# A two-layer graph kernel: every block transposed on VectorE, 2 MB loads in 1,024-byte runs, interleaved row sets

## The reference, cut to what matters

```python
def L0(x, evals, evecs, t):                    # evecs is adj, 4096 x 4096
    x_spec = einsum('nk,nc->kc', evecs, x)     # adj^T x
    coefs = exp(-evals * clip(t[0], 1e-8))[:, None]
    return einsum('nk,kc->nc', evecs, coefs * x_spec)   # adj (coefs * adj^T x)
def L1(inputs, adj, W, b):
    adj_hat = adj + eye(N)
    return tanh((adj_hat / adj_hat.sum(1)) @ (inputs @ W) + b)
x = layernorm(x + L0(x, evals, adj, t))        # x: 4096 x 128, float32
x = layernorm(x + L1(x, adj, W, b))
```

## Time and profile before

| | |
|---|---|
| median of 3 runs | 701.69 us (701.64 to 701.8) |
| the profiled execution, its own time | 704.87 us |
| its span | 703.1 us |
| busy: PE, DVE, ACT, POOL | 636.9, 516.4, 407.2, 341.6 us |
| DMA, whole span | 176.82 MB, 251 GB/s |

### The profile page before, as it was taken

The page is one execution under the profiler, slowest core; times in us unless marked ns, Lnnn a source line. Parts: engine busy times, 40 slices in busy tenths (PEclk is TensorE's granted clock), DMA queues, the critical chain, the costliest instruction groups (busy, mean ns, idle before and its releaser), DMA issues.

```text
span 703.1 us, 9318 instructions
## 1 busy us (share of the span) xinstructions
PE 636.9 (91%) x3016; PEld 518.7 (74%) x3016; DVE 516.4 (73%) x648; ACT 407.2 (58%) x825; POOL 341.6 (49%) x167
## 2 busy tenths in 40 slices
PE   3899999999958779899998999999999799898983
PEld 3688888887747558677786888888888587777862
DVE  3699899998949787868774356465528589698975
ACT  4899999999944555535453435346325364554540
POOL 0000000002916677664929848767927738373751
PEclk9999999999988999999998999999999899999997
DMA  8999999999999999897969759788749789999900
GB/s 290 387 386 386 387 387 387 387 387 387 332 248 248 231 270 220 237 190 216 252 155 274 172 128 241 179 180 241 184 115 267 152 224 262 240 264 266 255 16 30
DMA packets 198582, 176.82 MB, mean 251 GB/s; under 512 B 6280, under 2 KB 147848, under 8 KB 198544
## 3 DMA queue, kind: packets, MB, share of 16 engines
q1 hardware_dynamic: 124080, 137.90, 65.3%
q10 hardware_dynamic: 74464, 38.43, 24.8%
HBM read 174.21 MB, written 2.10 MB: 251 GB/s over the span
## 4 chain that ended last, share of the span: by engine, by line
PE 49%; POOL 13%; DVE 12%; ACT 10%; issue 7%; DMA 4%; ACTq 4%; SPq 0%; POOLq 0%; DVEq 0%
POOL lo L320 11%; PE ps L659 10%; PE ps L661 10%; PE ps L660 10%; ACT hi L358 7%; PE ps L652 5%; DMA raw<-in_adj_dram 4%; PE ps L630 4%; PE ps L632 4%; PE ps L631 4%; DVE vt L474 3%; DVE lo L482 3%; ACTq L261 3%; ACT hi L373 2%; POOL rstd L315 1%
## 5 line engine op out<-in xcount | busy, mean ns | idle before, releaser
L320 POOL TENSOR_TENSOR lo<-vt,hi 128x1024 fp32r<-128x1024 f32 x119 | 296.8, 2524 | 166.9 <-ACT hi L373 166.9
L474 DVE STREAM_TRANSPOSE vt<-raw 128x1024 f32<-128x1024 f32 x138 | 167.8, 1229 | 58.8 <-PE ps L661 57.6
L373 ACT ACTIVATE hi<-vt 128x1024 fp32r<-128x1024 f32 x138 | 142.2, 1057 | 71.5 <-DVE vt L474 50.6
L455 DVE TENSOR_TENSOR lo<-raw,hi 128x1024 fp32r<-128x1024 f32 x120 | 154.4, 1287 | 21.6 <-ACT hi L358 19.1
L358 ACT ACTIVATE hi<-raw 128x512 fp32r<-128x512 f32 x256 | 158.5, 622 | 14.4 <-DMA raw<-in_adj_dram 8.7
L373 ACT ACTIVATE hi<-ps 128x1024 fp32r<-128x1024 f32 x62 | 63.4, 1028 | 116.1 <-PE ps L652 114.1
L659 PE MATMUL ps<-hi,s_hi 128*128 128x512 f32 x256 | 108.7, 425 | 8.2 <-POOL lo L320 7.9
L482 DVE TENSOR_TENSOR lo<-ps,hi 128x1024 fp32r<-128x1024 f32 x62 | 75.0, 1211 | 54.2 <-ACT hi L373 54.1
L630 PE MATMUL ps<-hi,xg_hi 128*128 128x512 f32 x256 | 102.8, 402 | 9.5 <-DVE lo L455 8.7
L659 PE MATMUL ps<-hi,p_hi 128*128 128x512 f32 x256 | 105.4, 412 | 4.2 <-POOL lo L320 3.1
L308 POOL TENSOR_TENSOR lo<-raw,hi 128x1024 fp32r<-128x1024 f32 x8 | 25.4, 3197 | 169.4 <-ACT hi L358 169.3
(11 more groups left out here) (60 smaller groups left out, 611.3 us busy)
## 6 DMA issues: line engine op xcount, KB each, us to landing
raw<-in_adj_dram SPq DMA_DIRECT2D x95, 1024.0 KB, 14.2
raw<-in_adj_dram SPq DMA_DIRECT2D x138, 256.0 KB, 5.6
raw<-in_adj_dram ACTq DMA_DIRECT2D x138, 256.0 KB, 6.4
out_dram<-o_g ACTq DMA_DIRECT2D x8, 256.0 KB, 3.7
x_sb<-in_x_dram SPq DMA_DIRECT2D x1, 1792.0 KB, 14.7
x_sb<-in_x_dram SPq DMA_DIRECT2D x1, 256.0 KB, 3.3
w_sb<-in_L_gnn_W_dram ACTq DMA_DIRECT2D x1, 64.0 KB, 6.1
b_bc<-in_L_gnn_b_dram ACTq DMA_DIRECT2D x1, 64.0 KB, 8.0
```

What stands on the lines that cost most here:

```text
L320: nc.gpsimd.tensor_tensor(lo[:, slot(p), :], vt[:, slot(p), :], hi[:, slot(p), :].bitcast(f32), ALU.subtract).then_inc(pool_lo_ready, 1)
L373: nc.scalar.activation(hi[:, slot(s), :], src, ACT.Copy).then_inc(hi_ready, 1)
L455: nc.vector.tensor_tensor(lo[:, q % RING1, :], raw[:, k, 2 * h:2 * h + 2, :].rearrange("p r n -> p (r n)"), hi[:, q % RING1, :].bitcast(f3 ...
L474: nc.vector.transpose(vt[:, slot(s), :].rearrange("p (m b i) -> p m b i", m=2, b=RB), raw[:, BLOCKS[n].buf].rearrange("p r w -> p (r w)") ...
```

## The change

Five things change together. (1) PE transposes no block of adj any more: DVE transposes all 200 steps, and lo of every step is made from `vt` in SBUF, by DVE for 55 steps and by POOL for 145. (2) Loads are of 2 MB: 512 rows by 1,024 columns, 52 of them for 100 blocks, in 3 buffers in place of 6 of 1 MB, in runs of 1,024 bytes. Where only one half of the columns is needed (rows of odd groups in stage 3, four times), the whole 2 MB are loaded. (3) A row group takes every other set of 32 rows of 1,024 rows, and a column unit every other set of 32 columns of 1,024, so `x`, `out` and the spectrum are laid out anew; x is loaded by 8 DMAs. (4) All loads of adj are issued by SP, four quarters in a row. (5) Stage 3 writes its results over `x_sb`, without the buffer `o_g` and its wait. Besides, in the last visit of stage 1 POOL makes lo of 4 of the 16 halves, not of 8, and the spectrum is transposed in pairs of chunks, the last pair behind the products of step 1. The row groups are taken from 0 up.

```diff
-    BY_TENSOR = (0, 1)
-    RAW_RING = 6
+    BUFS = 3
+    WQ = 2 * CW // QN
...
     def on_vector(s):
-        if block(s).by_tensor:
-            return True
-        n = V_STEPS.index(s)
-        return n % 4 == 3 if block(s).spectral and block(s).visit < 4 else n % 6 == 5 and not block(s).spectral
+        if STEP[s].spectral:
+            return s % 16 in (2, 5, 8, 11, 14) if STEP[s].group < 3 else s % 4 == 2
+        return s % 7 in (2, 5)
...
+    LATE_POOL = [q for q in range(PAIRS) if q % 4 == 1]
+    LATE_DVE = [q for q in range(PAIRS) if q % 4 != 1]
...
-    adj_q = adj.rearrange("(g b n) (k q w) -> g k q n b w", b=RB, n=QP, q=QN, w=P)
+    adj_q = adj.rearrange("(v a e n) (u q w) -> v e u q n a w", v=NU, e=2, n=QP, q=QN, w=WQ)
...
-            for n in range(NB):
+            for n in range(NL):
                 wait_buffer(sp, n)
-                if BLOCKS[n].by_tensor:
-                    sp.dma_start(raw[:, BLOCKS[n].buf], adj_v[group(BLOCKS[n].visit), BLOCKS[n].col])\
-                        .then_inc(raw_in[BLOCKS[n].buf], 16)
-                else:
-                    load_quarters(sp, n, (0, 1))
+                load_quarters(sp, n, range(QN))
...
             def hi_step(s):
-                wait_turned(act, s)
+                act.wait_ge(vturned, s + 1)
                 wait_slot(act, s)
-                src = turn_slot(s).rearrange("p a n -> p (a n)") if block(s).by_tensor else vt[:, slot(s), :]
-                nc.scalar.activation(hi[:, slot(s), :], src, ACT.Copy).then_inc(hi_ready, 1)
-                n = AFTER.get(s // 2)
-                if s % 2 == 1 and n is not None and not BLOCKS[n].by_tensor:
-                    load_quarters(act, n, (2, 3))
+                nc.scalar.activation(hi[:, slot(s), :], vt[:, slot(s), :], ACT.Copy).then_inc(hi_ready, 1)
...
-            for p in range(1, POSITIONS):
-                if p + AHEAD < STEPS and not block(p + AHEAD).by_tensor:
+            for p in range(AHEAD, POSITIONS):
+                if p + AHEAD < STEPS:
                     turn_step(p + AHEAD)
...
+            def spectrum(u):
+                pe.wait_ge(spec_out, 2 * u + 2)
+                for c in range(2 * JB):
+                    last = nc.tensor.transpose(ps[:, 2 * u + c // JB, c % JB * C:(c % JB + 1) * C],
+                                               spec[:, u % 2, c * P:(c + 1) * P], ident[:, :])
+                last.then_inc(sT_done, 1)
...
-            for p in range(2, POSITIONS):
-                if p < STEPS and block(p).by_tensor:
-                    turn_step(p)
+            for p in range(AHEAD, POSITIONS):
                 if 0 <= p - LAG < STEPS:
                     products(p - LAG)
+                if p - LAG == 1:
+                    spectrum(NU - 1)
```

More of the change, by code:

```diff
@@ L7 @@
 @dataclass(frozen=True)
-class Block:
-    visit: int
-    col: int
+class Load:
+    group: int
+    wide: int
     buf: int
-    by_tensor: bool
+@dataclass(frozen=True)
+class Step:
+    load: int
+    last_of_load: bool
+    group: int
+    unit: int
+    half: int
     spectral: bool
@@ L90, in spectral_then_graph_conv, with wides2 @@
[L90 to L100, removed]
+    def wides2(g):
+        newest = (g - 1) // 2 if g else NU - 1
+        known = [u for u in range(NU) if 2 * u + 1 < g and u != newest]
+        unknown = [u for u in range(NU) if 2 * u + 1 >= g and u != newest]
+        order = []
+        while known or unknown:
+            if unknown:
+                order.append(unknown.pop(0))
+            if known:
+                order.append(known.pop(0))
+        return order + [newest]
@@ L102, in on_vector @@
+    NL = len(LOADS)
+    STEP = [Step(n, w == WORK[n][-1] and half == 1, LOADS[n].group, w[0], half, w[1], w[2], w[3])
+            for n in range(NL) for w in WORK[n] for half in range(2)]
+    STEPS = len(STEP)
+    BEFORE = [next((m for m in range(n - 1, -1, -1) if LOADS[m].buf == LOADS[n].buf), None) for n in range(NL)]
+    LAST_STEP = [max(s for s in range(STEPS) if STEP[s].load == n) for n in range(NL)]
     def on_vector(s):
-        if block(s).by_tensor:
-            return True
-        n = V_STEPS.index(s)
@@ L114, in spectral_then_graph_conv @@
     LO_BY_POOL = {s: i + 1 for i, s in enumerate(POOL_LO)}
-    END2 = [max(s for s in range(STEPS) if block(s).spectral and block(s).visit == v) for v in range(NG)]
-    END3 = [max(s for s in range(STEPS) if block(s).row == r) for r in range(NG)]
+    LATE_POOL = [q for q in range(PAIRS) if q % 4 == 1]
+    LATE_DVE = [q for q in range(PAIRS) if q % 4 != 1]
+    END2 = [max(s for s in range(STEPS) if STEP[s].spectral and STEP[s].group == g) for g in range(NG)]
+    END3 = [max(s for s in range(STEPS) if STEP[s].row == r) for r in range(NG)]
@@ L570, in ending3 @@
                         dve.wait_ge(sumT_done, row - 1)
-                    nc.vector.tensor_tensor(stage[:, par, :], acc_row(row), save(v), ALU.add).then_inc(sum3, 1)
+                    nc.vector.tensor_tensor(stage[:, par, :], acc_row(row), save(g), ALU.add).then_inc(sum3, 1)
                 if since == 2:
@@ L663, in products @@
             def products(s):
-                bl = block(s)
-                v = bl.visit
-                first = FIRST[v, bl.row] == s
-                final = s == (END2[v] if bl.spectral else END3[bl.row])
+                st = STEP[s]
+                g = st.group
+                first = FIRST[g, st.row] == s
+                final = s == (END2[g] if st.spectral else END3[st.row])
                 wait_lo(pe, s)
-                if bl.spectral and v == 0:
-                    pe.wait_ge(s_ready, max(bl.col + 1, 5))
```

411 lines of the change are left out of this document (181 added, 230 removed).

## The result

The change makes the kernel slower: 853.74 us (median of four runs, 847.89 to 859.4) against 701.66 beside it, a ratio of 1.217 (95% interval 1.207 to 1.227). Forecast were 690 us, in a range of 674 to 718. The profiled execution took 849.83 us with a span of 848.0.

A forecast was written before the change was run, and what follows sets the result against it. PE was taken to bound late stage 2, POOL's stalls its earlier visits, PE and DVE stage 3. Handover -4, stage 2 -18 and stage 3 +10 gave -12: 704.9 becomes 693, the median 690 us, range 674 to 718.

The forecast's parts named there:

- Stage 1 ... is the same program over the same 2,048-byte runs, and I leave it at no change.: Stage 1 before 170 us, limited by its loads: same program and run length, so no change in time.
- A packet of 1,024 bytes then costs 44 to 75 ns, a load 5.6 to 9.6 us; I take 7.5.: Loads in stage 3: 7.5 us each against 4 steps of 2.2, hidden but for four loads, which add 2 us.
- Four issues of 0.49 us are no limit for SP: Stage 3 loads: SP issuing all four quarters, at 0.49 us an issue, does not limit the kernel.
- The rival: Loads or PE's clock become the bound; loads at 75 ns a packet add about 25 us, 727 us; together chance 0.08.
- signs that the prediction named for being wrong: Subtractions from `vt` over 2.5 us, DVE's transpositions waiting for DMA, or stage 3's clock under 0.9.
- Stage 2, -18: Groups 1 to 7: 287.8 us before become 269.8, a gain of 18, with ends of 25 and 6.
- the floor of 262.3: Groups 1 to 7: sum of each group's largest engine time among DVE, POOL and PE, before added waits: 262.3 us.
- Stage 3, +10: Stage 3: 153.1 us before become 163, a loss of 10, between 1 and 27; DVE the bound, POOL beside it.
- 94% share of DVE: Stage 3: DVE, with 151.5 us of work, is busy 94% of the time, giving 161 us.
- The rival of shared ports: All 200 subtractions on DVE and POOL stand in one queue; stage 3 +20, in all +14, 716 us; chance 0.22.
- Handover, -4: Handover and group 0, 79.1 us before: a gain of 4, between a gain of 10 and a loss of 4.
- The even order brings all of its bounds: Rival summing -10, -25 and +1 for handover, stage 2 and stage 3: 668 us; chance 0.1.

## Why the prediction was wrong

The forecast gave faster and 690; the result is slower by 152 us. By its steps:

**"Stage 1 ... is the same program over the same 2,048-byte runs, and I leave it at no change."** This step failed, and it is the larger part: 118 to 123 us by three kernels. The diff turns the view `(g p r)` into `(u a e h r)`, which reaches the 128 partitions as 16 sets of 8; the prediction looked at the run's length and not at how 128 partitions are reached. It put the term at nothing, and the stage loaded at 225 GB/s in place of 377. Bounds for a changed access were due here too, and the kernel before held none for this one: all its chunk loads had one even step.

**"A packet of 1,024 bytes then costs 44 to 75 ns, a load 5.6 to 9.6 us; I take 7.5."** The second failure, 48 to 56 us. 2.1 MB at 213 GB/s are 9.8 us, a little beyond the upper end. The price was worked out by bytes in a packet from a kernel where two queues wrote both halves; what matters is which partitions are written at one time. "Four issues of 0.49 us are no limit for SP" was right in itself and beside the point: the move from two queues to one was priced as SP's time, never as the loss of the second half. The rival came close for this part: 727 us, where the change with stage 1 undone took 731 and 736; it had 0.08. Its 75 ns a packet (2.1 MB in 9.8 us are 77) had been worked out from bytes alone, so the number was near by luck. Two of the signs that the prediction named for being wrong did come: the transpositions waited 109.3 us for loads, and the clock in stage 3 was 0.86.

**Stage 2, -18.** Right in mechanism; -29.5 measured with loads that keep up (258.3 us, below even the floor of 262.3; the forecast was 269.8). The floors of groups 5 to 7, 38.2, 41.0 and 43.7 us, were met by 38.2, 40.8 and 43.6, with PE always busy. The added 7.5 us for waits were too much, as were 2.3 us a subtraction: 2.13 measured (65.9 us for 31).

**Stage 3, +10.** +1.1 measured (154.2 us, loads that keep up). The 94% share of DVE was right (146.18 of 154.2, 95%). The subtraction was not: priced at 2.15, it took 1.82 us (36.5 us for 20), and so DVE had 146.2 us for 151.5. (Its own terms, 125.85 and 27, give 152.9; and DVE makes 56 of the 200 subtractions and POOL 144, not 55 and 145, with 20 of DVE's in stage 3, not 19.) That half of POOL's instruction is waited for whenever POOL is at work was too strict: with POOL busy 84% in stage 2 and 91% in stage 3 the durations went from 1.17 to 3.34 us, with the lower mean in the busier stage. The rival of shared ports falls: single subtractions passed its 2.6 us, no stage's mean did.

**Handover, -4.** -0.6 measured. The clock stood at 0.89 from 170 to 248.5.

**The small edits** (x in eight loads, results over `x_sb`, strides of the transposition) cost nothing that shows: transpositions took 1,190 to 1,248 ns, and with the rows together stage 1 loads 377 GB/s up to 170 us, as the kernel before did.

With the loads mended the engines' part is -29 us (675.23 against 704.29), where the sum had -12: right in sign and too cautious, and nearer the rival "The even order brings all of its bounds" (-34, chance 0.1). The loads' part is about +178 (853.74 less 675.23). The 0.2% that the prediction gave as the least difference that can be told was too narrow: the kernel before spread over 2%, 695.87 to 709.91 us.

## What to carry to other kernels

When a diff changes a transfer, write down for old and new which partitions are written at the same time, by which queue, and into how many sets the partitions fall if they are not reached in one even step (32 and 64 sets ran at full speed here, 16 and 8 did not); the same bytes in the same runs ran here at 363 or 127 GB/s by that alone, over the whole phase. Look at the stages that "stay the same" for accesses whose view was rewritten. And when work is taken off a bounding engine, work out the load rate that the faster stage needs and compare it with what its queues give.

## What was new of the hardware

- A load over 128 partitions in 2,048-byte runs, over whole phases: 366 GB/s with one even step, 363 with 32 sets (64 sets took as long), 216 for 16 sets and 127 for 8, at a DMA share of 1.00, 0.99, 1.03 and 0.52. Inside a phase one even step gives 387.
- Loads of 64 partitions: 82.6 and 84.5 us in either half, 47.0 across the middle, for 16.78 MB.
- Two queues that write different halves: 347 GB/s inside a phase with 1,024-byte runs, 290 with 512. In the same half, 75.3 us in place of 53.0. From one queue, runs of 512, 1,024 and 2,048 bytes take 78 to 82 us alike.
- Sixteen sets of rows read alike whether they lie 40 or 128 rows apart (74.7 to 80.7 us); whole loads with 4,096-byte runs reach 410 GB/s inside a phase.
